# Edge stage of a graph network's first layer: every other running sum carried by TensorE

## The reference, cut to what matters

```
q = (feat @ Wq.T + bq).reshape(n, H, D)          # H = 4 heads of D = 64
k, v likewise
e = einsum('ehd,ehd->eh', q[src], k[dst]) * scale
ex = exp(e - segment_max(e, dst)[dst])
sa = ex / segment_sum(ex, dst)[dst]
agg = segment_sum(sa[:, :, None] * v[src], dst)
```

## Time and profile before

| | us |
|---|---|
| median of 3 runs | 6235.39 |
| the profiled execution's own time | 6232.7 |
| its span | 6230.8 |
| VectorE busy over the span | 3982.9 (64%) |
| TensorE matmuls busy | 4655.4 (75%) |
| ScalarE busy | 2668.4 (43%) |
| GpSimd busy | 3080.8 (49%) |

### The profile page before, as it was taken

The page is one execution under the profiler, slowest core; times in us unless marked ns, Lnnn a source line. Parts: engine busy times, 40 slices in busy tenths (PEclk is TensorE's granted clock), DMA queues, the critical chain, the costliest instruction groups (busy, mean ns, idle before and its releaser), DMA issues. The chain is left out here.

```text
span 6230.8 us, 86151 instructions
## 1 busy us (share of the span) xinstructions
PE 4655.4 (75%) x21453; PEld 3370.4 (54%) x21454; DVE 3982.9 (64%) x9527; ACT 2668.4 (43%) x5421; POOL 3080.8 (49%) x3260
## 2 busy tenths in 40 slices
PE   6977577777777697499999225566556659999999
PEld 4753255555555597366666215444444436666665
DVE  6864389999999777232222777777777764444443
ACT  1541055555555432154444212767776632222222
POOL 2767366666666487577777001777777720000000
PEclk7989899989899855599999557777777779999999
DMA  2014678888888686333232227555555530000000
GB/s 57 1 28 119 227 236 250 249 249 246 250 248 251 205 200 166 99 80 79 65 79 66 77 64 232 154 151 149 151 151 150 150 102 12 12 12 12 5 7 12
DMA packets 587385, 787.21 MB, mean 126 GB/s; under 512 B 207700, under 2 KB 427323, under 8 KB 586749
## 3 DMA queue, kind: packets, MB, share of 16 engines
q0 software_dynamic: 159136, 383.90, 23.0%
q1 hardware_dynamic: 290173, 351.82, 17.8%
q10 hardware_dynamic: 137972, 50.36, 3.3%
HBM read 634.22 MB, written 158.32 MB: 127 GB/s over the span
## 5 line engine op out<-in xcount | busy, mean ns | idle before, releaser
L1372 POOL DMA_INDIRECT b_got<-tmp_l_table,b_src x928 | 878.6, 947 | 505.8 <-issue 256.2
L2473 POOL DMA_INDIRECT w_got<-tmp_l_table,w_src x928 | 881.9, 950 | 284.4 <-issue 277.2
L3216 POOL DMA_INDIRECT t_got<-tmp_f_table,t_src x672 | 634.4, 944 | 220.4 <-issue 202.7
L1616 PE MATMUL b_pk<-b_keys,b_hot_t 128*128 x1856 | 532.9, 437 | 249.7 <-issue 157.2
L2736 PE MATMUL w_pa<-w_got,w_hot 128*128 128x264 f32 x1856 | 589.7, 471 | 98.8 <-DVE w_got L2643 96.5
L1616 PEld LDWEIGHTS b_pk<-b_keys,b_hot_t 128*128 128x128 f32 x1856 | 377.8, 214 | 335.2 <-issue 280.8
L3667 DVE SCALAR_TENSOR_TENSOR l_accs<-l_po,l_prob,l_accs 128x256 f32 (+1 forms) x392 | 173.5, 480 | 566.8 <-PE l_po L3776 566.8
L3719 ACT ACTIVATE l_h<-l_ph,l_bn 128x896 f32<-128x896 f32 x224 | 245.0, 1096 | 655.6 <-PE l_ph L3766 655.6
L2736 PEld LDWEIGHTS w_pa<-w_got,w_hot 128*128 128x128 f32 x1856 | 406.2, 231 | 205.2 <-issue 120.3
L1631 PE MATMUL b_pa<-b_got,b_hot 128*128 128x260 f32 x1856 | 487.7, 410 | 5.6 <-DVE b_acc L1543 4.8
L1631 PEld LDWEIGHTS b_pa<-b_got,b_hot 128*128 128x128 f32 x1856 | 387.0, 209 | 77.4 <-issue 7.0
(11 more groups left out here) (579 smaller groups left out, 9980.2 us busy)
## 6 DMA issues: line engine op xcount, KB each, us to landing
tmp_g_acc<-b_acc SPq DMA_DIRECT2D x232, 260.0 KB, 3.6
b_spread<-tmp_g_rel_rows SPq DMA_DIRECT2D x116, 256.0 KB, 5.3
w_spread<-tmp_g_rel_rows SPq DMA_DIRECT2D x116, 256.0 KB, 3.5
e_attr<-in_edge_attr ACTq DMA_DIRECT2D x103, 256.0 KB, 4.4
tmp_f_experts<-t_y SPq DMA_DIRECT2D x28, 896.0 KB, 4.5
t_spread<-tmp_f_rel_rows SPq DMA_DIRECT2D x174, 128.0 KB
yl_y<-tmp_f_experts SPq DMA_DIRECT2D x20, 896.0 KB, 11.2
b_got<-tmp_l_table,b_src POOLq DMA_INDIRECT x928, 4.5
```

The source lines that it names most:

```text
L1372: pool.indirect_dma_start(out=got[:, m % NB, u, :], out_offset=None, in_=T["l0_table"], in_offset=bass.IndirectOffsetOnAxis(ap=src[:, m * ...
L1616: mm = pe.matmul(pk[:, b % 2, u * D:(u + 1) * D], hot_t[:, (at * B4 + b) % HB, u * P:(u + 1) * P], keys[:, bass.ds(tile[u // 2], 1), :], s ...
L2473: pool.indirect_dma_start(out=got[:, p % 3, u, :], out_offset=None, in_=T["l1_table"], in_offset=bass.IndirectOffsetOnAxis(ap=src[:, p * R ...
L3216: pool.indirect_dma_start(out=got[:, g % RING, u, :], out_offset=None, in_=T["f_table"], in_offset=bass.IndirectOffsetOnAxis(ap=src[:, g * ...
```

## The change

The running sums of even stops stay as they were, adds on VectorE. For an odd stop TensorE adds the running sum of the stop before it into the bank itself, by a third multiplication: the identity times the sum in SBUF (`carry_of_stop`). ScalarE then copies the bank into `acc` (`collect`). Where an odd stop starts a new node tile, the multiplication reads a tile of zeros; which of the two is read is a register value, worked out from `keep` by VectorE during the setting up. The numbers lie in a new row, `orders`, beside the tile numbers of the round, so the register load of a round has 12 values in place of 8. `added` is now counted by VectorE and ScalarE by turns, `summed` of an odd stop by its carry. The fade of the last sum moves behind the spans. The carry of a round's last stop comes after `expand` of batch 1 in the round after next, its copy at the head of ScalarE's round. TensorE's start waits for the setting up.

```diff
+    FADED, NONE = AS, AS + 1
...
+        orders = s.sb("orders", [1, ROUNDS + 2, RS + RS // 2], I32)
...
-        acc = s.sb("acc", [P, AS, WV])
-        faded_acc = s.sb("faded_acc", [P, WV])
+        sums = s.sb("sums", [P, AS + 2, WV])
+        acc, faded_acc = sums[:, 0:AS, :], sums[:, FADED, :]
...
+            sp.dma_start(orders[0:1, 0:ROUNDS - 2, 0:RS], T[L.name + "_i_row"][RS + 2:RS * (ROUNDS - 1) + 2]
+                         .rearrange("(a p s) -> a p s", a=1, s=RS)).then_inc(loaded, 16)
+            sp.dma_start(orders[0:1, ROUNDS - 2, 0:RS - 2], T[L.name + "_i_row"][RS * (ROUNDS - 1) + 2:L.stops]
+                         .rearrange("(a s) -> a s", a=1)).then_inc(loaded, 16)
...
+            def collect(p, n):
+
+                g = p * RS + n
+                act.wait_ge(summed, g + 1)
+                act.activation(acc[:, n % AS, :], pa[:, n % 2, 0:WV], ACT.Copy).then_inc(added, 1)
...
+                if two_behind:
+                    collect(p - 2, RS - 1)
...
                     make_apart(p - 1, 3)
+                collect_of(1)
                 if two_ahead:
                     make_hot_t(p + 2, at + 2, 1)
...
                     make_apart(p, 0)
+                collect_of(3)
+                if now_:
...
                     load_masks(act, p + 1)
+                collect_of(5)
...
-            dve.wait_ge(loaded, 64)
+            dve.memset(sums[:, NONE, :], 0.0)
+            dve.wait_ge(loaded, 96)
+            for n in range(1, RS, 2):
+                before = (n - 1) % AS
+                behind = n // (RS - 1)
+                dve.tensor_scalar(orders[0:1, 1 + behind:ROUNDS + 1 + behind, RS + (n // 2 + 1) % (RS // 2)], keep[0:1, :].rearrange("a (p s) -> a p s", s=RS)[:, :, n],
+                                  float(before - NONE), float(NONE), ALU.mult, ALU.add)
...
-            def add(p, at, n):
+            def add(p, n):
 
                 g = p * RS + n
                 if n == 0:
                     dve.wait_ge(faded, p + 1)
                 else:
                     dve.wait_ge(added, g)
-                if n % 2 == 0 and (not isinstance(p, int) or p or n >= AS):
+                if not isinstance(p, int) or p or n >= AS:
                     dve.wait_ge(stored[n // 2 % 2], 16 * (RS // AS * p + n // AS))
                 dve.wait_ge(summed, g + 1)
...
-                    add(p - 2, at - 2, RS - 2)
-                    add(p - 2, at - 2, RS - 1)
-                if behind:
-                    fade_last(p - 1)
+                    add(p - 2, RS - 2)
                 score_of(0)
                 if now_:
                     spans(p)
+                if behind:
+                    fade_last(p - 1)
                 weigh_of(1)
-                adds(0, 1)
+                add_of(0)
                 weigh_of(2)
                 if now_:
                     chains(p)
                 score_of(1)
-                adds(2, 3)
+                add_of(2)
                 weigh_of(3)
                 if now_:
                     differences(p)
                 score_of(2)
-                adds(4, 5)
+                add_of(4)
...
+            def orders_of(p, a, b):
+
+                return values(orders[0:1, bass.ds(p, 1), a:b].rearrange("a p s -> a (p s)"))
...
+            def sum_of_stop(p, n, k):
+
+                g, b = p * RS + n, n // 2
+                pe.wait_ge(hot_ready, p * B4 + b + 1)
+                pe.wait_ge(rhs_ready, p * B4 + b + 1)
+                if not isinstance(g, int) or g >= 2:
+                    pe.wait_ge(added, g - 1)
+                for u in range(2):
+                    v = 2 * (n - 2 * b) + u
+                    mm = pe.matmul(pa[:, n % 2, 0:WV], hot[:, b, v, :], got[:, k, v, D:ROW], start=(u == 0), stop=(n % 2 == 0 and u == 1))
+                if n % 2 == 0:
                     mm.then_inc(summed, 1)
+
+            def carry_of_stop(p, n, value):
+
+                before = nc.s_assert_within(value, 0, NONE, skip_runtime_bounds_check_because="it is worked out from a comparison's 0 or 1")
+                pe.wait_ge(added, p * RS + n)
+                pe.matmul(pa[:, n % 2, 0:WV], K["ident"][:, :], sums[:, bass.ds(before, 1), :], start=False, stop=True).then_inc(summed, 1)
...
+                last = RS + RS // 2 if behind else RS + 1 if two_behind else RS
+                if two_ahead and (two_behind or not behind):
+                    found = orders_of(p, 0, last)
+                    tile, before = found[0:RS], found[RS:]
+                else:
+                    if ahead:
+                        tile = orders_of(p, 0, RS if two_ahead else RS - 2)
+                    skip = 0 if two_behind else 1
+                    before = [None] * skip + list(orders_of(p, RS + skip, last))
                 expand_of(1)
-                sums_of(0, 0, 1)
+                if two_behind:
+                    carry_of_stop(p - 2, RS - 1, before[0])
+                sum_of(0)
+                sum_of(1)
                 if now_:
                     chain_ends(p)
                 expand_of(2)
-                sums_of(1, 2, 3)
+                carry_of(1)
+                sum_of(2)
+                sum_of(3)
                 if now_:
                     spread_tops(p)
                 expand_of(3)
-                sums_of(2, 4, 5)
+                carry_of(3)
+                sum_of(4)
+                sum_of(5)
                 if now_:
                     turn_weights(p)
                 expand_of(4)
-                sums_of(3, 6, 7)
-
-            pe.wait_ge(loaded, 64)
+                carry_of(5)
+                sum_of(6)
+                sum_of(7)
...
+            pe.wait_ge(set_up, 2)
+            pe.wait_ge(loaded, 96)
             pe.wait_ge(keys_in[0], 16)
-            tile = tiles(0, 0, 10)
+            tile = values(i_row[0:1, 0:RS + 2])
```

More of the change, by code:

```diff
@@ L1554, in score_of, with add_of @@
                         score(p + 1, at + 1, b, slot(at + 1, b), turn + (B4 * (at + 1) + b) // NB)
-                def adds(*stops):
+                def add_of(n):
                     if behind:
-                        for n in stops:
-                            add(p - 1, at - 1, n)
+                        add(p - 1, n)
                 if behind:
```

56 lines of the change are left out of this document (25 added, 31 removed).

## The result

The changed kernel takes 6147.27 us (median of 4 runs, 6144.47 to 6164.77), the kernel before in the same set 6235.28 us (4 runs, 6229.11 to 6241.73). The ratio is 0.9865, with a 95% interval from 0.9844 to 0.9886. The forecast was 6203 us: the sign was right, the gain is 2.7 times as large as forecast (88 us in place of 32), and the time lies within the range, but the gain does not come by the forecast's sum. A second set on another chip gave 0.9891, 0.9875 to 0.9908.

What follows compares the result with a forecast made beforehand. VectorE was taken as the bound at 23.88 us a round; a new ring of 22.1 us plus 1.2 for low clock gives 23.23, 0.65 less in 56 rounds: -36, edges +4, median +2.7, 6203 us; range 6130 to 6275.

Steps and rivals of the forecast that it cites:

- VectorE's part: VectorE in a round: gives up four adds at 0.69 us, 2.76 us in all, and then needs 20.6 us without waits.
- TensorE's carries: TensorE: four identity multiplications a round, 0.46 us each at full clock, 1.84 us a round; 0.74 each at the low level.
- ScalarE's copies: ScalarE: four copies a round out of the sum's bank, 0.40 us each plus 0.1 to hand over.
- The new ring: TensorE and ScalarE wait in turn: expand(1), carry(7), copy(7), six preparations, copy(1), sum(3) to next turning, load; 22.1 us at full clock.
- Turning and register load: TensorE at a round's head: 2.41 + 0.93 = 3.34 us, about 1.1 hidden behind the last sums, 2.24 us left.
- sum(3) to the next turning: TensorE from the sum of stop 3 to the next turning of the scores, without a pause: 10.2 us at full clock.
- low level: TensorE at 1.2 GHz: expand(1) takes 3.57 in place of 1.84 us, 1.7 us more, in 7 rounds of 10.
- the edges: First and last rounds and start: small loads on SyncE 1 us, last round's add, carry and copy 3 us; +4 us in all.
- rival (c): Low clock in every round, with a second pause ahead of sum(3): 23.8 us a round, 6230 to 6242 us; chance 15%.
- Two signs: Copy(7) on ScalarE waits 3 to 5 us, under 2 refuting the predicted chain; VectorE waits 1 to 2 us ahead of the fade.
- Rival (b): Register values cost 0.07 us each: load 0.9 us, ring at most 20.5, VectorE bounds; about 6054 us; chance 12%.
- Rival (a): Register load does not begin before TensorE's array is idle: rounds 24.4 to 24.9 us, about 6281 us; chance 25%.

Runs made afterwards that it cites:

- the early copy: Changed kernel with ScalarE's copy of stop 1 moved ahead of the last three of its six preparations: 6056.47 us, ratio 0.9696 to the kernel before.
- the late load: Changed kernel whose TensorE sequencer waits until the scores are turned before loading its 12 register values: 6150.52 us, ratio 0.9845 to the kernel before.

## Why the prediction was off, step by step

- **VectorE's part: right.** It was to give up 2.76 us a round and need 20.6. With the early copy it is the bound at 20.4 us.
- **TensorE's carries: right.** A carry takes 0.60 us as its rows are printed, and 0.44 with the overlap taken off (1410.61 to 1411.05); 0.46 was predicted.
- **ScalarE's copies: a little too dear.** 0.36 to 0.39 us, where 0.40 plus 0.1 was taken.
- **The new ring: right in its course.** Copy(7) waits for carry(7), the six preparations stand behind it, copy(1) behind those, and sum(3) waits for copy(1), 119.4 us in 1100 us. The early copy confirms it.
- **Turning and register load, 2.24 us left: this step failed.** It measured 0.65 us in the mean. The prediction went by the line's slope of 0.233 us a value and added four values at that price, 1.94 + 0.93 = 2.86 us. But the change doesn't read the tile that the kernel before reads. It reads rows of its own in `orders`, and from there the load of 12 takes 0.85 us in two rounds of three, 0.07 us a value, the price of ScalarE's load, which the prediction used as a bound for the four new values only. Such a load is wholly hidden behind the last sums, and expand(1) starts 0.24 us behind the turning. In the third round it takes 1.5 to 1.8 us, and expand(1) starts 0.9 to 1.7 us behind the turning; what makes it longer there is open. That the place of the values makes the load short is shown twice: rows of their own, put into the kernel before, make its load 0.59 us and the kernel 29 us faster; the old start of a row, put into the changed kernel, makes the load 3.26 us.
- **The sum, part by part.** The two rounds shown above, from one turning to the next, and the means of 45 rounds in us (from the start times of the same rows; the last column is the late load):

| part of the ring | predicted | at 1408.54 | at 1432.15 | mean | late load, mean |
|---|---|---|---|---|---|
| turning to expand(1) | 2.24 | 0.24 | 1.42 | 0.65 | 2.02 |
| expand(1) to copy(7) | 2.30 | 2.47 | 2.46 | 2.46 | 2.58 |
| copy(7) to copy(1) | 6.8 | 7.42 | 6.59 | 7.18 | 6.59 |
| copy(1) to sum(3) | 0.5 | 0.42 | 0.41 | 0.42 | 0.42 |
| sum(3) to the next turning | 10.2 | 13.06 | 9.92 | 11.97 | 10.69 |
| low level, by itself | 1.19 | in the above | none | in the above | in the above |
| round | 23.23 | 23.61 | 20.80 | 22.68 | 22.30 |

The load's term was 1.6 us too long. Against it stand 0.9 us more for the low level (11.97 - 9.92 = 2.05 in place of 1.19) and 0.5 us in which ScalarE's preparations wait for their rows to spread, which the prediction did not have: in this trace they do so only in rounds where expand(1) starts 0.24 us behind the turning. The rest is 0.3 us of small parts. So the forecast's round was 0.55 us too long, which is the remainder of larger errors that go against each other.
- **The terms are not independent.** The late load puts about the predicted 2.0 us back, and the round becomes shorter still, 22.30 us: the spreading rows are no longer waited for, and the stretch behind sum(3) falls by 1.3 us. So the wrong size of the load's term is shown, but that term alone does not explain the missing time on this kind of chip.
- **The miss of 56 us.** 0.55 us in 56 rounds are 31 us, the edges 4, and 20 us lie outside the profile: the sum puts the median 2.7 us above the profiled execution, and it lay 17.5 us below it.
- **The low level: its share right, its place and price wrong.** 7 rounds in 10 were taken; 34 of 45 have it, wholly or in part. It was to come behind the pause ahead of expand(1) at 1.7 us; it comes behind the pause ahead of sum(3), where the stretch up to the turning takes 13.06 in place of 9.92 us, all of it in the ring. The second pause was named in rival (c).
- **Two signs failed.** By the prediction the ring would be wrong if copy(7) waited less than 2 us; it waits 1.7 us in the mean (1.33 and 2.52 us in the two rounds), not 3 to 5, and the fade 0.2 us, not 1 to 2. Yet the early copy shows the ring. Both signs rested on the late expand(1), and with the late load both are about met (3.2 and 1.0 us). VectorE's own waits are 2.0 us a round, as that sign asked.
- **Rival (b)** had the price of a value right for two rounds of three, but put the ring at "at most 20.5", without the second pause and its low level, and so its 6054 us lies by what the early copy gives (6056), not by what the change gives. **Rival (a)** asked whether the load begins before the array is idle: it does, at 1407.5 us (duration in ns, first and last start of two loads), while TensorE's last sums run until 1408.7.

```profile
L1633 PEldq TENSOR_LOAD <-b_orders x2: 851/1177/1503, 1407.5 to 1431.7; - x2
```

The Trainium skill, page "TensorE: Matmul & The Clock Gate", section "Architectural detail: the array is 16× 32×32, not 1× 128×128", gives TensorE a queue of 64 instructions. The row above agrees that the sequencer is ahead of the array, here with a register load. The Trainium skill, page "Runtime: NRT & Kernel Launch", section "Instruction fetch mechanics", gives about 200 ns a register for a TENSOR_LOAD. Here it was 0.07 us in two rounds of three and 0.12 to 0.15 in the third from the new rows, and 0.24 to 0.27 us from rows that begin at their third word, so the measurements differ from it in both directions.

- **Edges**: nothing is left for them in the 67.9 us; +4 us was predicted.

## What to carry over

When a change reads the same values from a new tile, don't carry the old row's price over: price the new layout, and where the trace has the same instruction at two prices (here 0.23 and 0.07 us a value), find out what tells the two apart before choosing. When a gain is off by a factor, try the by-products of the change alone: here where the values lie was worth 29 us in the kernel before, beside a gain of 67 on the same chip. And measure the parts, not only the total: a forecast that is 0.55 us a round off hid a term that was 1.6 us off. A term put back need not take the time back, since another may shrink with it. When the trace shows an engine in order waiting behind work that nobody needs soon, move the handed-on result ahead of it: one moved line was worth more (122 us) than the change itself (67 to 88 us).

## What the runs showed of the hardware

- The time of a register load of TensorE differs with the rows that it reads: rows that begin on multiples of 12 words gave 0.59 us for 8 values and 0.85 for 12; rows that begin at the third word of 8 or of 16 gave 1.94 us for 8 and 3.26 for 12 (medians). Start and width of a row were changed together, so which of them decides, and whether the rule is one of 4, 8 or 16 words, is not shown. Nor is it the only thing: from the same rows 15 of 49 loads of the changed kernel took 1.48 to 1.83 us, and the median was 1.15 us with the early copy and 1.2 us with the late load.
- TensorE's sequencer issues a register load while the array still works on matmuls of before: the load begins at 1407.5 us, and the array goes on until expand(1) at 1408.78 without a gap.
- The low level came behind pauses of 2.73 and 2.95 us. Behind pauses of 1.83 and 1.89 us in one round with the late load expand(3) was slow, 3.44 us; behind 1.75 and 1.90 us in the round before it was not. In the kernel before with rows of its own a group behind pauses of 0.92 and 0.75 us was slow too (3.44 in place of 1.99 us). So the length of the last pause doesn't decide alone:

```profile
1434.25 0.33 PE L1647 MATMUL b_px<-const_ident,b_one 128*128 128x128 f32 x1 [0.92 <-DVE b_one L1482]
1435.32 3.44 PE L1627 MATMUL b_pk<-b_keys,b_hot_t 128*128 x8 [0.75 <-ACT b_hot_t L1392]
```

- Two kinds of chips gave this one change opposite signs, 0.9865 and 1.0045. A verdict holds for the chip that gave it.
